# A gated cross-attention block: fills of the first and last batch reordered, and the query gathers issued by ScalarE

## The reference

```python
x = x + tanh(g_xattn) * attention(layernorm(x), ctx, ctx)     # x: 16 x 224 x 512, ctx: 16 x 750 x 512
x = x + tanh(g_ffn) * ffn(layernorm(x))
# attention: q = query @ Wq.T * 32**-0.5, k = key @ Wk.T, v = value @ Wv.T, 16 heads of 32
scores = sigmoid(einsum('blhd,bshd->bhls', q, k))
o = einsum('bhls,bshd->blhd', scores, v) @ Wo.T
# ffn: 8 experts, each on 2 of the 16 batches: gelu(t @ w1 + b1) @ w2 + b2, d_ff = 2048
```

## Time and profile before

| | |
|---|---|
| median of 3 runs | 1662.09 us |
| profiled execution, own time | 1662.63 us |
| its span in the trace | 1661.0 us |
| TensorE busy | 1648.9 us (99%) |
| ScalarE busy | 797.0 us (48%) |
| VectorE busy | 805.6 us (49%) |
| granted TensorE clock, mean | 0.998 |

### The profile page before, as it was taken

The page is one execution under the profiler, slowest core; times in us unless marked ns, Lnnn a source line. Parts: engine busy times, 40 slices in busy tenths (PEclk is TensorE's granted clock), DMA queues, the critical chain, the costliest instruction groups (busy, mean ns, idle before and its releaser), DMA issues.

```text
span 1661.0 us, 30322 instructions
## 1 busy us (share of the span) xinstructions
PE 1648.9 (99%) x11460; PEld 1454.9 (88%) x11460; DVE 805.6 (49%) x1388; ACT 797.0 (48%) x1087; POOL 176.0 (11%) x261
## 2 busy tenths in 40 slices
PE   9899999999999999999999999999999999999999
PEld 8788888888888888888888888999999999999998
DVE  6444443443543443444444334664646555555544
ACT  5555555555555555555555546333333333433332
POOL 2111111111112021121111120000000000000000
PEclk9999999999999999999999999999999999999999
DMA  8777777787786787777777776535354453526241
GB/s 274 216 216 207 211 225 208 194 223 201 197 238 185 213 223 187 214 213 201 213 212 192 218 223 165 183 124 182 124 183 137 143 178 102 182 98 218 101 169 49
DMA packets 195691, 309.03 MB, mean 186 GB/s; under 512 B 27088, under 2 KB 153616, under 8 KB 195568
## 3 DMA queue, kind: packets, MB, share of 16 engines
q1 hardware_dynamic: 173632, 229.43, 49.5%
q0 software_dynamic: 21936, 77.94, 13.5%
HBM read 228.44 MB, written 78.84 MB: 185 GB/s over the span
## 4 chain that ended last, share of the span: by engine, by line
PE 96%; DMA 2%; DVE 1%; ACT 1%; issue 0%; SPq 0%; POOL 0%; ACTq 0%; POOLq 0%; DVEq 0%
PE fill_ps L686 32%; PE scores_ps L872 19%; PE fill_ps L853 13%; PE scores_ps L728 10%; PE heads_ps L745 8%; PE fill_ps L695 6%; PE heads_ps L853 5%; PE fill_ps L696 3%; DMA k_st<-k_scr 0%; PE heads_ps L822 0%; DMA x_mr<-stat_scr 0%; DMA k_scr<-k_stage 0%; DMA q_st<-q_scr 0%; PE scores_ps L695 0%; SPq L404 0%
## 5 line engine op out<-in xcount | busy, mean ns | idle before, releaser
L872 PE MATMUL scores_ps<-ctx_hl,wK 128*128 128x448 f32 x1536 | 316.6, 362 | 0.0
L872 PEld LDWEIGHTS scores_ps<-ctx_hl,wK 128*128 128x128 f32 x1536 | 288.1, 188 | 19.8
L686 PE MATMUL fill_ps<-ctx_hl,wK 128*128 128x500 f32 (+1 forms) x1560 | 287.5, 334 | 0.0
L686 PE MATMUL fill_ps<-wV,ctx_hl 128*125 128x512 f32 x1152 | 281.6, 395 | 0.2 <-DVE k_stage L1199 0.2
L686 PEld LDWEIGHTS fill_ps<-ctx_hl,wK 128*128 128x128 f32 x1560 | 236.2, 189 | 31.2 <-issue 5.4
L686 PEld LDWEIGHTS fill_ps<-wV,ctx_hl 128*125 128x125 f32 x1152 | 209.6, 186 | 48.1 <-DVE k_stage L1199 0.4
L853 PE MATMUL fill_ps<-wQ,wV 128*128 128x448 f32 x1152 | 243.4, 365 | 0.0
L853 PEld LDWEIGHTS fill_ps<-wQ,wV 128*128 128x128 f32 x1152 | 216.0, 188 | 17.2 <-issue 0.4
L911 ACT ACTIVATE probs<-scores_ps 125x896 f32<-125x896 f32 x192 | 176.8, 921 | 89.0 <-PE scores_ps L728 57.2
L728 PE MATMUL scores_ps<-q_st,k_st 96*125 96x224 f32 x1536 | 201.8, 274 | 2.6 <-DMA q_st<-q_scr 1.3
L728 PEld LDWEIGHTS scores_ps<-q_st,k_st 96*125 96x125 f32 x1536 | 188.7, 189 | 17.4 <-issue 6.1
(11 more groups left out here) (120 smaller groups left out, 1709.7 us busy)
## 6 DMA issues: line engine op xcount, KB each, us to landing
k_st<-k_scr SPq DMA_DIRECT2D x576, 125.0 KB, 4.0
v_sb<-w_in SPq DMA_DIRECT2D x92, 512.0 KB, 4.6
k_scr<-k_stage POOLq DMA_DIRECT2D x62, 500.0 KB, 4.6
ctx_raw<-ctxT_in SPq DMA_DIRECT2D x48, 500.0 KB, 4.8
q_st<-q_scr SPq DMA_DIRECT2D x192, 112.0 KB, 4.2
k_scr<-k_stage POOLq DMA_DIRECT2D x68, 250.0 KB, 4.3
probs<-w_in SPq DMA_DIRECT2D x32, 512.0 KB, 3.6
q_scr<-q_stage POOLq DMA_DIRECT2D x64, 224.0 KB, 5.2
```

The source lines that it names most:

```text
L686: last = pe.matmul(out_, lhsT(kt, a), rhs(kt, c), start=(kt == 0 and t == 0), stop=(kt == KT - 1 and t == 2))
L872: last = pe.matmul(y_ps[:, dt, 0:T], w2[:, slot, a, k, dt * P:(dt + 1) * P], hid_hl[:, slot, d, k, :], start=(c == 0 and k == 0 and t == 0 ...
```

## The change

Four things. (1) `gather_q` moves from SP to ScalarE. Tiles 1, 2 and 3 stay at steps 0, 3 and 6, behind the sigmoids, the square and `o_hi` of the step, ahead of its fills. Tile 0 of the next batch goes from step 10 of SP to step 11 of ScalarE, behind that step's two sigmoids; for batch 0 it goes to step 9 of `b` = -1, ahead of `square(-1)`. (2) In batch 0 V 4 moves to the end of FILL_FIRST, V 5 to step 1, Q 7 from step 2 to 3, V 0 ahead of Q 0, and Q 0 from step 7 to 8. `load_mr(1)` stands ahead of `load_ctx(1, ..., 2)`, and `moments(-1)` ahead of the last `w_lo`. (3) In the last batch K 5 moves from step 7 to 5. (4) `e_hi`/`e_lo` of the first expert's third w1 tile move from step 11 to 10, those of its first w2 tile behind `o_hi`/`o_lo`.

```diff
     FILL_FIRST = [(0, "K", 6), ... (10, "Q", 2),
-                  (11, "V", 3)]
+                  (11, "V", 3), (11, "V", 4)]
-    FILL_0 = [(0, "K", 0), (1, "V", 4), (2, "K", 2), (2, "Q", 7), (3, "V", 5), (4, "K", 3), (5, "K", 5)] + [
-        f for f in FILL if f[0] > 6 or f[1:] == ("K", 6)]
+    FILL_0 = [(0, "K", 0), (1, "V", 5), (2, "K", 2), (3, "Q", 7), (4, "K", 3), (5, "K", 5), (7, "K", 6), (7, "V", 0),
+              (8, "Q", 0)] + [f for f in FILL if f[0] > 7 and f[1:] != ("V", 0)]
     FILL_LAST = [...
-                 (4, "V", 4), (5, "V", 5), (7, "K", 5)]
+                 (4, "V", 4), (5, "V", 5), (5, "K", 5)]
 # SP, in body(b, h, par)
-                    if attends(b) and s in (0, 3, 6):
-                        gather_q(b, s // 3 + 1)
-                    if prepares(b) and s == 10:
-                        gather_q(b + 1, 0)
+                    if s == 5 and known(b, 0):
+                        load_mr(1)
                     if attends(b) and prepares(b) and s in (1, 2, 5):
                         load_ctx(b + 1, nh, npar, {1: 0, 2: 1, 5: 2}[s])
...
-                    if s == 5 and known(b, 0):
-                        load_mr(1)
 # ScalarE (gather_q itself is as before, with act in the place of sp)
                     if s == VISIT and attends(b):
                         o_hi(b, 0)
+                    if attends(b) and s in (0, 3, 6):
+                        gather_q(b, s // 3 + 1)
+                    if attends(b) and prepares(b) and s == 11:
+                        gather_q(b + 1, 0)
                     for kind, i in fills_at(b, s):
...
                     if known(b, -1):
+                        if s == 9:
+                            gather_q(0, 0)
                         for which in folds_at(b, s):
                             square(b, which)
...
+                        if s == 10:
+                            e_hi(0, 1, 2)
                         if s == 11:
-                            e_hi(0, 1, 2)
                             gelu(0, 0)
-                            e_hi(0, 2, 0)
+                    if known(b, B) and s == 0:
+                        e_hi(0, 2, 0)
 # VectorE
+                    if known(b, 0) and s == 1:
+                        moments(-1)
                     if known(b, 0):
                         for n in W_LO.get(s + STEPS, ()):
                             w_lo(n)
-                    if known(b, 0) and s == 1:
-                        moments(-1)
```

More of the change, by code:

```diff
@@ L72, in flamingo_block @@
     FILL_FIRST = [(0, "K", 6), (1, "K", 9), (2, "V", 0), (3, "V", 1), (4, "K", 7), (5, "K", 10), (6, "T", 0), (6, "T", 1),
-                  (7, "V", 2), (8, "Q", 0), (9, "Q", 1), (9, "K", 8), (10, "K", 11), (10, "Q", 2), (11, "V", 3)]
-    FILL_0 = [(0, "K", 0), (1, "V", 4), (2, "K", 2), (2, "Q", 7), (3, "V", 5), (4, "K", 3), (5, "K", 5)] + [
-        f for f in FILL if f[0] > 6 or f[1:] == ("K", 6)]
+                  (7, "V", 2), (8, "Q", 0), (9, "Q", 1), (9, "K", 8), (10, "K", 11), (10, "Q", 2), (11, "V", 3), (11, "V", 4)]
+    FILL_0 = [(0, "K", 0), (1, "V", 5), (2, "K", 2), (3, "Q", 7), (4, "K", 3), (5, "K", 5), (7, "K", 6), (7, "V", 0),
+              (8, "Q", 0)] + [f for f in FILL if f[0] > 7 and f[1:] != ("V", 0)]
     FILL_LAST = [(0, "K", 0), (1, "K", 2), (1, "O", 0), (1, "O", 1), (2, "V", 2), (2, "V", 3), (3, "K", 3), (3, "O", 2), (3, "O", 3),
-                 (4, "V", 4), (5, "V", 5), (7, "K", 5)]
+                 (4, "V", 4), (5, "V", 5), (5, "K", 5)]
     K_FILLS = 2 * KT
@@ L405, in gather_k @@
                                  scr["k"][j % RING, half].rearrange("(j p) s -> p j s", p=HD)).then_inc(s_k_in[r], 16)
[L407 to L414, removed]
             def load_w(n):
@@ L891, in _, with gather_q @@
         def _(act):
+            def gather_q(n, mt):
+                r = mt % 2
+                alone(act, s_q_st[mt], 16 * (n + 1))
+                alone(act, s_scores, STEPS * n + 3 * (mt - 2) + 3)
+                for t, half in enumerate((HI, HI, LO)):
+                    act.dma_start(q_st3[t * HD:(t + 1) * HD, r].bitcast(F32),
+                                 scr["q"][mt, half].rearrange("(j p) l -> p j l", p=HD)).then_inc(s_q_in[r], 16)
             def ctx_hi(n, h, par, c):
@@ L1261, in body @@
                     if known(b, B - 1):
-                        if s == 11:
+                        if s == 10:
                             e_lo(0, 1, 2)
-                            e_lo(0, 2, 0)
                     if known(b, B) and s == 0:
+                        e_lo(0, 2, 0)
                         split_hidden(0, 0)
```

## The result

| | before | after |
|---|---|---|
| median of 4 runs | 1661.9 us | 1751.44 us |
| profiled execution | 1662.63 us | 1755.32 us |
| its span | 1661.0 us | 1753.6 us |
| TensorE busy | 1648.9 us (99%) | 1685.8 us (96%) |
| mean granted clock | 0.998 | 0.975 |

The kernel is slower: ratio 1.0529, 95% interval 1.0513 to 1.0545. One of the four runs of the kernel after (2058.07 us, mean clock 0.749) and one of the eleven of the kernel with only the first gather on ScalarE (4535.82 us) were disturbed and are left out of the ratios, while the median of 1751.44 above still holds the first of them: the other three took 1746.16, 1747.57 and 1755.32 us. 1675.5 us was forecast (1657 to 1696): the sign is right, the loss six to seven times too small.

What follows compares the result with a forecast made beforehand. TensorE, 99% busy, was taken as the bound, so only its idle time and clock matter. 1662.6 − 7.35 (batch 0) + 1.03 (first gather) + 20.1 (tile 0) − 0.9 (last batch) = 1675.5 us, range 1657 to 1696.

Steps and rivals of the forecast that it cites:

- Tile 0 at step 11: Batch ends: tile 0 issued on ScalarE lands after its need, stalling TensorE 1.5 us per batch, +20.1 us in sum.
- The upper bound: Tile 0's landing at batch ends: at most 5.2 us, as the last of the keys, giving a stall of 2.5.
- the third rival: Tile 0's gather: the DMA waits for more than a semaphore, all 1.3 us later; 1695, with low clock above 1700; 12%.
- the late issue: Tile 0's gather: ScalarE issues only when its sigmoid has ended (598.24), 1.3 us later; 1695 us.
- two queues in each other's way: Tile 0's gather: SP's and ScalarE's queues hinder each other while both issue, all 1.3 us later; 1695 us.
- Batches 0 and 14: Tile 0 without the means' load in the slot: keys take 2.9 us, stall 0.2 to 0.3 us each.
- The reading of the sequencer: ScalarE at step 11: sequencer holds until an instruction's semaphore comes, then is free; first DMA goes out at 597.0.
- The stall for `xnT`: Batch 0, first query fill: TensorE's 4.25 us wait for normalised input goes, and the low clock with it, −7.35 us.
- a risk of up to 3 us: Front, first gather: 2.5 us idle before V 4 may lower the clock, costing up to 3 us beyond the counted +1.03.
- The reason given for the stall: Batch 0: SP issues the means' load only at 56.52, because the context load ahead of it waits until 55.65.
- Steady gathers of tiles 1 to 3: Steps 0, 3, 6: gathers take ScalarE's sequencer 1.3 us, free under its idle time; tiles wanted three steps later.
- Last batch: K 5 earlier removes a 1.05 us gather wait, w1 delay costs 0.5, moved weights return 0.3; together −0.9 us.

Runs made afterwards that it cites:

- the run with tile 0 early: Kernel after, with only the gather of tile 0 of batches 1 to 15 back on SP at step 10; 1659.12 us, ratio to before 0.9985.

## Why the prediction was wrong

**The step that failed** is the landing in "Tile 0 at step 11": "I take 1.5, since the row with 165 issues of the very transfer is the nearest". The 165 gathers of the earlier trace rows were taken from all places in a batch, tile 0 among them, which at its old place had landed 4.44 us after its first issue (batch 8, DMA share 0.85). The one moved went to the place where SP issues the keys of step 2, right behind the means; what these would do to it, and it to them, was in no term of the sum. Forecast: third issue 0.87 us after the first, then 4.2 us, 5.1 us in all; measured 8.06 in the median, a stall of about 4 us in 14 of 15 batches instead of 1.5. The upper bound, 5.2 us of the keys, was a bound only for the load as it was; the gather itself adds three transfers to it. The keys beside the queries now take 6.6 us at most (5.2 before).

**The low clock** was named in the third rival ("A stall of 3 us or more may also bring the low clock each time, and then it is above 1700", 12%), and that rival comes nearest: not by the late issue, and not by two queues in each other's way either, since one queue does the same (1753.02), but by the transfers. It took them for 1.3 us; they cost 3.0 (8.06 against 5.1). In the window above TensorE's matmuls are 37.67 us longer for the clock, a term that the sum had at nothing. With the keys held back there are 14 stalls of up to 2.7 us; the clock fell after 4 of them (2.75, 2.44, 1.93 and 1.78 us) and held after the others, 1.82 us among them:

```profile
288.93 1.13 PE L717 MATMUL scores_ps<-q_st,k_st 96*125 96x224 f32 x8 [1.82 <-DMA q_st<-q_scr]
289.99 4.75 PE L734 MATMUL heads_ps<-probs,v_sb 125*32 125x224 f32 x96
...
484.45 1.13 PE L717 MATMUL scores_ps<-q_st,k_st 96*125 96x224 f32 x8 [1.93 <-DMA q_st<-q_scr]
485.51 6.43 PE L734 MATMUL heads_ps<-probs,v_sb 125*32 125x224 f32 x96
```

With keys and means held back, 899 − 892.68 = 6.3 us of idle time in stalls up to 1.4 us left the clock at 1.00; in the kernel after all 14 stalls at step 0, 2.09 to 5.08 us, brought it down. So the price of a late transfer here is not one microsecond per microsecond: from 6.3 us of idle time to 53.1, matmul time goes from 892.68 to 927.67.

**Batches 0 and 14**, which have no means in the slot, were to stall 0.2 to 0.3 us. They stalled 2.09 and 3.34. In batch 14 tile 0 came 7.08 us after its first issue, and 3.35 with the keys held back: 3.7 us for the keys alone. In batch 0 it was 5.83 and 4.83, so something else holds it up there, which no run names. **Batch 1** was counted among the thirteen with the means in the slot; its means go out behind the gather, and it did not stall.

**The reading of the sequencer was right.** The gather is issued at 642.66, between the end of step 11's scores and the start of the sigmoid queued ahead of it. Its own conditions do not hold it: with the gather at step 10 it went out at 591.70, ahead of step 11's scores (594.19). The rule of the Trainium skill ("Perfetto Trace Analysis", DVE / Act Engine Instruction), by which it could be issued before the semaphore comes, does not hold in this row. Another page of the Trainium skill would have helped: "DMA: Bandwidth & Descriptors", Issuing engines are not separate DMA queues, says that DMAs of all issuing engines run on the same 16 DMA engines and interleave. The runs agree: with the six transfers in one queue the kernel takes 1753.02 us, in two 1751.44.

**Batch 0.** The stall for `xnT` went as said (−7.35), with a cover of 1.66 us where 0.8 to 1.5 was forecast. Square 30.49, K 11's remainder 34.80, V 4 at 35.26: forecast 30.6, 34.9, 35.45. What was off is the clock after 2.5 us of idle time, given as a risk of up to 3 us and not counted: scores at 39.70 instead of 38.25, +1.45. The keys of step 6 came 1.15 us late, which nothing in the prediction had. Together −3.9 instead of −6.3 (the two make −3.7 of it). The reason given for the stall was right and more than enough: the load behind the context load has it by itself.

**Steady gathers of tiles 1 to 3** are free, as forecast (1659.12 against 1659.71).

**Last batch**: −0.9 was forecast. The delay of w1 was sized well (from the copy of V to the w1 load 3.80 us, 2.63 before: +1.17 against 1.2), its cost was not: the keys of step 8 behind it also lost the K 5 fill as cover (1.4 us, which stood between steps 7 and 8) and came 1.81 us late, more than the 1.05 removed. From the scores of step 2 to the first fill of 24 matmuls in the expert is 77.79 us, 77.24 before: +0.5.

The sum: −3.9 at the front, +90.8 in the window, +5.2 for the stall ahead of batch 15 and its low clock (1065.2 to the scores of step 2 at 1087.48 is 22.28 us, 978.3 to 995.37 was 17.07), +0.5: 92.6 us of span.

## What to carry to other kernels

A landing time belongs to a place, not to a transfer: before a DMA is moved, look at what is issued within its landing time at the new place and how full the DMA engines are there, and count the moved transfer's load on the others, as tile 1 shows, which came late when keys and means were moved. In these runs no gain came from issuing on another engine's queue (1659.12 us at best, 1655.62 with all gathers on SP); what the consumer has is the distance from issue to need, and that was cut here from 10.1 us (587.2 to 597.31 in the run with tile 0 early) to 3.8. Where TensorE has no idle time, a stall repeated in every batch can cost the lower clock on top. Of the kernels run, the best are the order of fills, its lists alone or the load of the means alone, 1655 to 1656 us, with all gathers where they were.

## What was not expected of the hardware

- A gather of three transfers (3 × 112 KB) landed in 3.44 us from its first issue with nothing of SP's beside it, in 5.42 behind the means (2 transfers), and in 8.06 with three gathers of keys (3 × 125 KB) at the same moment.
- Idle times of similar length do not treat the clock alike: after 1.31 us it held, after 2.43 us it fell, and with the keys held back it held after 1.82 us and fell after 1.78. With SP's late gather ahead of the keys it held after 2.64 us and fell after 1.87.
